# The normalised input's high and low halves are transposed by two transfers, and the products with the high half come first

## The chip, the core and the metric

One Trainium2 chip, one of its cores. The time is the device time of one execution in microseconds (us). Of a kernel that is run several times it is the median; the profile is of one execution by itself.

## What is computed

A layer of a vision tower over 64 batches of 128 tokens with 1024 channels. The token part (a state space kernel) gives h; around the change stands the attention:

```python
h = _L0_tok_ref(L0_tok_log_dt, L0_tok_Lambda, x, 1024)
h = h + _L0_attn_ref(_layernorm(h, axis=-1), L0_attn_Wq, L0_attn_Wk, L0_attn_Wv, L0_attn_Wo)
h = h + _L0_ffn_ref(_layernorm(h, axis=-1), L0_ffn_A, L0_ffn_B, L0_ffn_Wr, L0_ffn_br)
...
q = (x @ Wq).reshape(b, t, N_HEADS, HEAD_DIM).transpose(0, 2, 1, 3)
k = (x @ Wk).reshape(b, t, N_KV, HEAD_DIM).transpose(0, 2, 1, 3)
v = (x @ Wv).reshape(b, t, N_KV, HEAD_DIM).transpose(0, 2, 1, 3)
```

`_layernorm` is (x - mean) / sqrt(var + 1e-5). Then come a rotary embedding, causal softmax over 128 tokens in 32 heads with 8 key heads, the output projection Wo, and a low-rank feed forward with a router of 8.

## The kernel before, in words

The first stage (`s4_stage`) makes h of all batches in DRAM, as h0, and leaves the weights in SBUF, each as the sum of two 16-bit parts, high and low (`wq_hi`, `wq_lo`). It ends at about 260 us of the span. The second stage (`layer_stage`) runs over the 64 batches with a pipeline written out by hand: every engine has a function `body(i, odd)` that lists its steps for turn i, and `bodies` runs it for i from -3 to 66. A step names the batch it serves, so turn i works on batches i - 3 to i + 3 at once, and each engine takes its steps strictly in this order. Before a step, `reached(engine, semaphore, per, b, k)` waits until the semaphore stands at per x b + k. A step for a batch that doesn't exist is left out.

The way of batch b up to its products:

- SP loads h0 of the batch into `h_ln` (`load_ln`, L761); one buffer. It waits until both halves of the low part of batch b - 1 are made (`xl_done[0]`, L764).
- DVE takes the statistics (`norm1_stats`), ACT and DVE the root, ACT normalises in place (`norm_apply`) and writes the high part, the 16-bit copy, to `xs[0][:, 0, :]` (`x_high`, L1045). DVE writes the low part, what the copy leaves, to `xs[0][:, 1, :]` in two steps of 512 columns (`x_low`, L1195). Half 0 of batch i + 3 is DVE's last step of turn i, after `kv_rotate(i + 2)` and `q_rotate(i + 2, 0)`, which wait for TensorE's products of batch i + 2; half 1 is in the next turn.
- SP transposes both parts by one DMA of 128 x 2048 into `xt[odd]` (`x_transpose`, L779, issued at L785): blocks 0 to 7 of it are the high part, 8 to 15 the low one.
- TensorE multiplies: `kv` (L886) into the PSUM bank `pa`, `q_half` (L896) into `pb` and `pc`. Each is 24 products of 512 columns, in `products` (L849): for every k of 0 to 7 x_high w_hi, x_high w_lo and x_low w_hi. The body gives them out in ranges of k between other work: scores, values, the output projection `wo_half`, the feed forward.

Scores need `qt` and `kt`, the transposed queries and keys. The probabilities of a group of four heads go from ACT (`exps`) over POOL (`normalise`) to ACT (`p_high`) and POOL (`p_low`), both parts are transposed by SP (`p_transpose`, 128 x 1024, into `pt`), and TensorE multiplies them with the values.

All of the stage's DMAs are issued by SP, in one queue. Its turn, L824:

```python
def body(i, odd):
    load_res(i - 1)
    p_transpose(i - 1, 6)
...
    x2_transpose(i - 2)
    load_ln(i + 3)
    p_transpose(i, 2)
    p_transpose(i, 3)
    x_transpose(i + 2, odd)
    q_transpose(i + 1, 0)
    p_transpose(i, 4)
    p_transpose(i, 5)
    k_transpose(i + 1, 0)
    store(i - 3)
```

Of the kernel before, what the change touches and what calls it, by code (L numbers as in the profile page):

```python
# [26 lines left out]
KC = D // P  # L27
# [591 lines left out]
def layer_stage(nc, h0, out, W):  # L619
# [5 lines left out]
    with ExitStack() as ctx:  # L625
# [3 lines left out]
        def sem(name):  # L629
            return ctx.enter_context(nc.semaphore(name))  # L630
# [11 lines left out]
        xs = [sb(f"xs{i}", [P, 2, D], f16) for i in range(2)]  # L642
        xt = [sb(f"xt{i}", [P, 2 * KC, P], f16) for i in range(2)]
# [36 lines left out]
        pv_ps, pa, pb, pc, pd, tx = (ps(n) for n in ("pv_ps", "pa", "pb", "pc", "pd", "tx"))  # L680
# [2 lines left out]
        ln_in = sem("ln_in")  # L683
        res_in = sem("res_in")
        out_sent = sem("out_sent")
        xt_in = sem("xt_in")
        x2t_in = sem("x2t_in")
        qt_in = [sem(f"qt_in{i}") for i in range(2)]
        kt_in = [sem(f"kt_in{i}") for i in range(2)]
# [3 lines left out]
        kv_done = sem("kv_done")  # L693
        q_done = sem("q_done")
# [36 lines left out]
        def has(b):  # L731
            return not isinstance(b, int) or 0 <= b < NB

        def reached(eng, s, per, b, k=0):

            if isinstance(b, int):
                if b < 0 or per * b + k == 0:
                    return
                if b >= NB:
                    b, k = NB, 0  # L740
            eng.wait_ge(s, per * b + k)
# [13 lines left out]
        with nc.Block() as block:  # L755
            @block.sync
            def _(sp):
                def row(ap, b):
                    return ap[bass.ds(b, 1), :, :].rearrange("b t d -> (b t) d")

                def load_ln(b):  # L761
                    if not has(b):
                        return
                    reached(sp, xl_done[0], 2, b)  # L764
                    sp.dma_start(h_ln[:, :], row(h0, b)).then_inc(ln_in, 16)

                def load_res(b):
                    if not has(b):
                        return
                    reached(sp, h1_done, 2, b)  # L770
                    sp.dma_start(h_res[:, :], row(h0, b)).then_inc(res_in, 16)

                def store(b):
                    if not has(b):
                        return
                    reached(sp, h2_done, 2, b, 2)
                    sp.dma_start(row(out, b), h2[:, :]).then_inc(out_sent, 16)

                def x_transpose(b, odd):  # L779
                    if not has(b):  # L780
                        return
                    reached(sp, xl_done[0], 2, b, 2)
                    reached(sp, q_done, 2, b - 2, 2)
                    reached(sp, kv_done, 1, b - 2, 1)
                    sp.dma_start_transpose(xt[odd][:, :, :],  # L785
                                           xs[0][:, :, :].rearrange("p a d -> p (a d)")).then_inc(xt_in, 16)

                def x2_transpose(b):
                    if not has(b):
                        return  # L790
                    reached(sp, xl_done[1], 2, b, 2)
                    reached(sp, low_done, 1, b)
                    sp.dma_start_transpose(x2t[:, :, :],
                                           xs[1][:, :, :].rearrange("p a d -> p (a d)")).then_inc(x2t_in, 16)

                def q_transpose(b, half):
                    if not has(b):
                        return
                    reached(sp, qd_done, 2, b, half + 1)
                    reached(sp, s_done, G, b - 1, G // 2 * (half + 1))  # L800
                    heads = slice(H // 2 * half, H // 2 * (half + 1))
                    sp.dma_start_transpose(qt[:, heads, :],
                                           qs[:, heads, :, :, :].rearrange("p h a b d -> p (h a b d)")
                                           ).then_inc(qt_in[half], 16)

                def k_transpose(b, half):
                    if not has(b):
                        return
                    reached(sp, kd_done, 1, b, 1)
                    reached(sp, s_done, G, b - 1, G // 2 * (half + 1))  # L810
                    groups = slice(G // 2 * half, G // 2 * (half + 1))
                    sp.dma_start_transpose(kt[:, groups, :],
                                           ks[:, groups, :, :, :].rearrange("p g a b d -> p (g a b d)")
                                           ).then_inc(kt_in[half], 16)

                def p_transpose(b, g):
                    if not has(b):
                        return
                    reached(sp, pl_done, G, b, g + 1)
                    pb_, pg = group(b, g - RP)  # L820
                    reached(sp, pv_done, G // 4, pb_, pg // 4 + 1)
                    sp.dma_start_transpose(pt[g % RP][:, :, :], p16[g % 2][:, :]).then_inc(pt_in[g % RP], 16)
# [4 lines that stand above are left out]
                    p_transpose(i - 1, 7)  # L827
                    k_transpose(i, 1)
                    q_transpose(i, 1)
                    p_transpose(i, 0)  # L830
                    p_transpose(i, 1)
                    x2_transpose(i - 2)
                    load_ln(i + 3)
                    p_transpose(i, 2)
                    p_transpose(i, 3)
                    x_transpose(i + 2, odd)
                    q_transpose(i + 1, 0)
                    p_transpose(i, 4)
                    p_transpose(i, 5)
                    k_transpose(i + 1, 0)  # L840
                    store(i - 3)


                bodies(sp, body)
                sp.wait_ge(out_sent, 16 * NB)

            @block.tensor
            def _(pe):
                def products(bank, x, name, cols, k0, k1):  # L849

                    w_hi, w_lo = W[name + "_hi"], W[name + "_lo"]
                    for k in range(k0, k1):
                        pe.matmul(bank, x[:, k, :], w_hi[:, k, cols], start=(k == 0), stop=False)  # L853
                        pe.matmul(bank, x[:, k, :], w_lo[:, k, cols], start=False, stop=False)  # L854
                        last = pe.matmul(bank, x[:, KC + k, :], w_hi[:, k, cols], start=False, stop=(k == KC - 1))  # L855
                    return last

                def scores(b, g):
# [27 lines left out]
                def kv(b, odd, k0, k1):  # L886
                    if not has(b):
                        return
                    if k0 == 0:
                        reached(pe, h1_done, 2, b - 3, 1)  # L890
                        reached(pe, xt_in, 16, b, 16)
                    last = products(pa[:, :], xt[odd], "wkv", slice(0, 512), k0, k1)
                    if k1 == KC:
                        last.then_inc(kv_done, 1)

                def q_half(b, odd, half, k0, k1):  # L896
                    if not has(b):
                        return
                    if k0 == 0 and half == 0:
                        reached(pe, h1_done, 2, b - 3, 2)  # L900
                    if k0 == 0 and half == 1:
                        reached(pe, q_used, 2, b - 1, 2)
                    if k0 == 0:
                        reached(pe, xt_in, 16, b, 16)
                    last = products((pb, pc)[half][:, :], xt[odd], "wq",
                                    slice(512 * half, 512 * half + 512), k0, k1)
                    if k1 == KC:
                        last.then_inc(q_done, 1)

# [86 lines left out]
            def _(act):  # L996
# [48 lines left out]
                def x_high(w, b):  # L1045
                    if not has(b):
                        return
                    reached(act, ln_x[w], 1, b, 1)
                    reached(act, (xt_in, x2t_in)[w], 16, b)
                    A.activation(xs[w][:, 0, :], (h_ln, xn)[w][:, :], ACT.Copy).then_inc(xh_done[w], 1)  # L1050

                def q_high_a(b):
# [82 lines left out]
            def _(dve):  # L1135
# [59 lines left out]
                def x_low(w, b, half):  # L1195
                    if not has(b):
                        return
                    reached(dve, xh_done[w], 1, b, 1)
                    cols = slice(HALF * half, HALF * half + HALF)
                    V.tensor_tensor(xs[w][:, 1, cols], (h_ln, xn)[w][:, cols], xs[w][:, 0, cols],  # L1200
                                    ALU.subtract).then_inc(xl_done[w], 1)
# [259 lines left out]
```

## Time and profile before

| | |
|---|---|
| median of 3 runs | 2426.91 us (2426.84 to 2429.64) |
| profiled execution, its own time | 2428.1 us |
| its span | 2426.3 us |
| busy: TensorE (PE) | 2293.9 us, 95% |
| busy: VectorE (DVE) | 1983.9 us, 82% |
| busy: ScalarE (ACT) | 1835.2 us, 76% |
| busy: GpSimd (POOL) | 1711.2 us, 71% |
| DMA queue of SP, share of 16 engines | 92.0% |

PE is TensorE's matmul side, PEld its weight loads, SPq SyncE's queue of DMA issues. Busy is the time in which at least one instruction of the engine ran; matmuls overlap, so a matmul's duration (0.38 us) is longer than the distance to the next. The mean over the span mixes two stages, so it doesn't say what bounds either. The chain that ended last is TensorE for 68% of the span, in the pieces L853, L854 and L855, which are the lines of `products`, with 7% each for the banks pa and pb; ACT and DVE have 7% each. "Issue to landing" of a DMA runs from its issue on SP to its last byte; the span of the issue itself on SPq is separate, and with a full queue it is longer.

### The profile page before, as it was taken

To read this page: it belongs to the slowest core of one execution; us is meant where nothing else is said; L and a number is where in the kernel's file an instruction comes from. 1 tells how busy PE (TensorE), PEld (TensorE's weight loads), DVE (VectorE), ACT (ScalarE), POOL (GpSimd) and SP (SyncE) were. 2 spreads that over 40 slices of the span, in tenths; PEclk is the share of its full clock that TensorE was granted. 3 is DMA by queue.
4 is the path that set the end of the run, shared out by engine and by line. 5 is a ranking of instruction groups with operands and counts; after the bars stand their busy time and mean duration, and the time that the engine had idled before them with its cause. 6 is when DMAs were issued, how large, how long until landed. Compare 5 with 4: busy or idle time off the path is not lost.

```text
span 2426.3 us, 58560 instructions
## 1 busy us (share of the span) xinstructions
PE 2293.9 (95%) x18704; PEld 1247.0 (51%) x18704; DVE 1983.9 (82%) x7796; ACT 1835.2 (76%) x6270; POOL 1711.2 (71%) x1529
## 2 busy tenths in 40 slices
PE   2999589999999999999999999999999999999986
PEld 2777245555555555555555555555555555555543
DVE  8999468888888888888888888888888888888864
ACT  5988278777777777777777777777877777777773
POOL 1444187777777777777777777777777777777772
PEclk9999799999999999999999999999999999999998
DMA  2888489999999999999999999999999999999985
GB/s 76 263 253 235 114 149 179 190 186 183 190 185 184 186 190 186 181 189 188 186 182 188 186 180 189 190 181 190 187 187 182 186 191 181 190 190 186 181 163 110
DMA packets 1199524, 443.63 MB, mean 183 GB/s; under 512 B 1149552, under 2 KB 1151856, under 8 KB 1199216
## 3 DMA queue, kind: packets, MB, share of 16 engines
q1 hardware_dynamic: 1199216, 439.89, 92.0%
q8 instruction: 149, 2.44, 0.4%
q14 instruction: 159, 1.30, 0.2%
HBM read 87.42 MB, written 67.11 MB: 64 GB/s over the span
## 4 chain that ended last, share of the span: by engine, by line
PE 68%; ACT 7%; DVE 7%; DMA 3%; issue 3%; POOL 1%; SPq 0%; POOLq 0%; ACTq 0%; DVEq 0%
PE pb L853 7%; PE pa L853 7%; PE pb L854 7%; PE pb L855 7%; PE pa L854 7%; PE pa L855 7%; ACT pr L1005 5%; PE s_ps L867 4%; PE pc L854 4%; PE pc L855 4%; PE pc L853 4%; PE pv_ps L882 3%; DMA pt<-p 2%; PE pd L853 1%; PE pd L855 1%
## 5 line engine op out<-in xcount | busy, mean ns | idle before, releaser
L1005 ACT ACTIVATE pr<-pr,smin 128x128 f32<-128x128 f32 x2048 | 796.5, 391 | 191.1 <-DVE smin L1146 190.9
L1351 POOL TENSOR_TENSOR pr<-pr,rinv 128x512 f32<-128x512 f32 x512 | 577.6, 1138 | 358.4 <-DVE rinv L1154 347.2
L1359 POOL TENSOR_TENSOR p<-pr,p 128x512 f16<-128x512 f32 x512 | 590.7, 1159 | 115.5 <-ACT p L1015 109.2
L1146 DVE CUSTOM_DVE_ANT_0 pr<-s_ps,cst 128x128 f32<-128x128 f32 x2048 | 471.4, 287 | 150.2 <-POOL p L1359 108.2
L1015 ACT ACTIVATE p<-pr 128x512 f16<-128x512 f32 x512 | 320.0, 625 | 169.6 <-POOL pr L1351 147.9
L1005 ACT ACTIVATION_READ_ACCUMULATOR pr<-pr,smin 128x1 f32 x2048 | 386.4, 189 | 0.0
L612 PE MATMUL hps<-z,xw 128*128 128x256 f32 x848 | 194.1, 389 | 62.5 <-POOL xw L322 42.1
L853 PE MATMUL pa<-wkv_hi,xt 128*128 128x512 f16 x512 | 195.0, 381 | 27.4 <-DMA xt<-xs 27.4
L612 PEld LDWEIGHTS hps<-z,xw 128*128 128x128 f32 x848 | 163.1, 195 | 93.0 <-POOL xw L322 50.5
L867 PE MATMUL s_ps<-kt,qt 128*128 128x128 f16 x2048 | 199.1, 220 | 8.9 <-issue 4.5
L867 PEld LDWEIGHTS s_ps<-kt,qt 128*128 128x128 f16 x2048 | 149.5, 98 | 107.0 <-DVE smin L1146 5.7
L853 PE MATMUL pb<-wo_hi,ctx_t 128*128 128x512 f16 x512 | 195.1, 381 | 3.9 <-DVE rt_s L1212 1.9
L853 PE MATMUL pa<-wo_hi,ctx_t 128*128 128x512 f16 x512 | 195.3, 382 | 2.2 <-DVE ctx_t L1160 1.7
L853 PE MATMUL pb<-wq_hi,xt 128*128 128x512 f16 x512 | 195.6, 382 | 0.0
L854 PE MATMUL pb<-wq_lo,xt 128*128 128x512 f16 x512 | 195.5, 382 | 0.0
L855 PE MATMUL pb<-wq_hi,xt 128*128 128x512 f16 x512 | 195.3, 381 | 0.0
L854 PE MATMUL pa<-wkv_lo,xt 128*128 128x512 f16 x512 | 195.1, 381 | 0.0
L855 PE MATMUL pa<-wkv_hi,xt 128*128 128x512 f16 x512 | 195.1, 381 | 0.0
L854 PE MATMUL pa<-wo_lo,ctx_t 128*128 128x512 f16 x512 | 194.6, 380 | 0.0
L854 PE MATMUL pb<-wo_lo,ctx_t 128*128 128x512 f16 x512 | 194.6, 380 | 0.0
L855 PE MATMUL pb<-wo_hi,ctx_t 128*128 128x512 f16 x512 | 194.6, 380 | 0.0
L855 PE MATMUL pa<-wo_hi,ctx_t 128*128 128x512 f16 x512 | 194.5, 380 | 0.0
(192 smaller groups left out, 5559.4 us busy)
## 6 DMA issues: line engine op xcount, KB each, us to landing
h<-hout SPq DMA_DIRECT2D x128, 256.0 KB, 3.5
h_ln<-h SPq DMA_DIRECT2D x64, 512.0 KB, 4.2
h_res<-h SPq DMA_DIRECT2D x64, 512.0 KB, 4.6
out<-h SPq DMA_DIRECT2D x64, 512.0 KB, 3.2
pt<-p SPq DMA_TRANSPOSE x512, 3.9
xa<-x SPq DMA_DIRECT2D x16, 256.0 KB, 4.0
xb<-x SPq DMA_DIRECT2D x32, 128.0 KB, 3.7
wst<-wq SPq DMA_DIRECT2D x8, 512.0 KB, 5.7
```

The costliest lines, as they stand in the source:

```text
L612: last = pe.matmul(hps[t % 4][:, QROW * i:QROW * i + QROW], xw[w % XWR][:, t % WIN, 2 * i:2 * i + 2, :], z[g % ZR][:, 2 * (t % 2) + m, :], ...
L853: pe.matmul(bank, x[:, k, :], w_hi[:, k, cols], start=(k == 0), stop=False)
L854: pe.matmul(bank, x[:, k, :], w_lo[:, k, cols], start=False, stop=False)
L855: last = pe.matmul(bank, x[:, KC + k, :], w_hi[:, k, cols], start=False, stop=(k == KC - 1))
L867: last = pe.matmul(s_ps[g % 2][:, j * P:(j + 1) * P], qt[:, HG * g + j, :], kt[:, g, :], start=True, stop=True)
L882: last = pe.matmul(pv_ps[j * HD:(j + 1) * HD, to], v[:, g * HD:(g + 1) * HD], pt[g % RP][:, lo + j, :], start=(n == 0), stop=(n == 2))
L1005: last = A.activation(p, p, ACT.Exp, bias=smin[g % 2][:, j:j + 1], scale=-1.0, accum_out=rsum[g % 2][:, j:j + 1])
L1015: A.activation(p16[g % 2][:, 0:HG * P], pr[g % 2][:, :], ACT.Copy).then_inc(ph_done, 1)
L1146: V.tensor_tensor_reduce(pr[g % 2][:, cols], s_ps[g % 2][:, cols], mask, 1.0, 3e38, ALU.add, ALU.min, smin[g % 2][:, j:j + 1]).then_inc(ma ...
L1351: nc.gpsimd.tensor_tensor(p3, p3, rinv[g % 2][:, :].unsqueeze(2).broadcast_to([P, HG, P]), ALU.mult).then_inc(p_norm, 1)
L1359: nc.gpsimd.tensor_tensor(p[:, HG * P:], pr[g % 2][:, :], p[:, 0:HG * P], ALU.subtract).then_inc(pl_done, 1)
```

## The change

The transfer of 128 x 2048 becomes two of 128 x 1024, with a semaphore each (`xth_in`, `xtl_in`). The high one waits for `xh_done` in place of `xl_done`. Both stand on SP where the one stood. For `kv` and `q_half` a new function `x_products` takes the place of `products`: the same 24 products in another order, first the 16 with the high part (w_hi and w_lo for each k), then the 8 with the low part. The places in the body stay, with as many products each; product 0 waits for the high transfer, product 16 for the low one. ACT's `x_high` waits for the high transfer of the batch before, DVE's `x_low` now for the low one. `wo_half` and `low` still use `products`.

```diff
-        xt_in = sem("xt_in")
+        xth_in = sem("xth_in")
+        xtl_in = sem("xtl_in")
...
-                def x_transpose(b, odd):
+                def x_high_transpose(b, odd):
+                    if not has(b):
+                        return
+                    reached(sp, xh_done[0], 1, b, 1)
+                    reached(sp, q_done, 2, b - 2, 2)
+                    reached(sp, kv_done, 1, b - 2, 1)
+                    sp.dma_start_transpose(xt[odd][:, 0:KC, :], xs[0][:, 0, :]).then_inc(xth_in, 16)
+
+                def x_low_transpose(b, odd):
                     if not has(b):
                         return
                     reached(sp, xl_done[0], 2, b, 2)
                     reached(sp, q_done, 2, b - 2, 2)
                     reached(sp, kv_done, 1, b - 2, 1)
-                    sp.dma_start_transpose(xt[odd][:, :, :],
-                                           xs[0][:, :, :].rearrange("p a d -> p (a d)")).then_inc(xt_in, 16)
+                    sp.dma_start_transpose(xt[odd][:, KC:, :], xs[0][:, 1, :]).then_inc(xtl_in, 16)
...
-                    x_transpose(i + 2, odd)
+                    x_high_transpose(i + 2, odd)
+                    x_low_transpose(i + 2, odd)
...
+                def x_products(b, bank, x, name, cols, j0, j1):
+
+                    w_hi, w_lo = W[name + "_hi"], W[name + "_lo"]
+                    for n in range(3 * j0, 3 * j1):
+                        if n == 0:
+                            reached(pe, xth_in, 16, b, 16)
+                        if n == 2 * KC:
+                            reached(pe, xtl_in, 16, b, 16)
+                        k, w = (n // 2, (w_hi, w_lo)[n % 2]) if n < 2 * KC else (n - 2 * KC, w_hi)
+                        last = pe.matmul(bank, x[:, k if n < 2 * KC else KC + k, :], w[:, k, cols],
+                                         start=(n == 0), stop=(n == 3 * KC - 1))
+                    return last
...
-                        reached(pe, xt_in, 16, b, 16)
-                    last = products(pa[:, :], xt[odd], "wkv", slice(0, 512), k0, k1)
+                    last = x_products(b, pa[:, :], xt[odd], "wkv", slice(0, 512), k0, k1)
...
-                    if k0 == 0:
-                        reached(pe, xt_in, 16, b, 16)
-                    last = products((pb, pc)[half][:, :], xt[odd], "wq",
-                                    slice(512 * half, 512 * half + 512), k0, k1)
+                    last = x_products(b, (pb, pc)[half][:, :], xt[odd], "wq",
+                                      slice(512 * half, 512 * half + 512), k0, k1)
...
-                    reached(act, (xt_in, x2t_in)[w], 16, b)
+                    reached(act, (xth_in, x2t_in)[w], 16, b)
...
+                    if w == 0:
+                        reached(dve, xtl_in, 16, b)
```

SP's queue at the start of the second stage, batches 0 and 1, before:

```order
L765 DMA h_ln<-h 128x1024
L765 DMA h_ln<-h 128x1024 [waits xl_done0]
L785 DMA_TRANSPOSE xt<-xs 128x16x128 [waits xl_done0]
L765 DMA h_ln<-h 128x1024 [waits xl_done0]
L785 DMA_TRANSPOSE xt<-xs 128x16x128 [waits xl_done0]
L802 DMA_TRANSPOSE qt<-qs 128x16x128 [waits qd_done]
```

and now:

```order
L766 DMA h_ln<-h 128x1024
L766 DMA h_ln<-h 128x1024 [waits xl_done0]
L786 DMA_TRANSPOSE xt<-xs 128x8x128 [waits xh_done0]
L794 DMA_TRANSPOSE xt<-xs 128x8x128 [waits xl_done0]
L766 DMA h_ln<-h 128x1024 [waits xl_done0]
L786 DMA_TRANSPOSE xt<-xs 128x8x128 [waits xh_done0]
L794 DMA_TRANSPOSE xt<-xs 128x8x128 [waits xl_done0]
L810 DMA_TRANSPOSE qt<-qs 128x16x128 [waits qd_done]
```

Each transpose is two, the first waits for the high part alone, and the load of h_ln that waits for the low part stands ahead of both, as it stood ahead of the one.

TensorE's queue, batch 0, the rows up to the first uses of the low part (31 products are ahead of the first row that waits for xtl_in, none of which reads the low part), now:

```order
L876 MATMUL pb<-wq_hi,xt 128x512
L876 MATMUL pb<-wq_lo,xt 128x512
L876 MATMUL pb<-wq_hi,xt 128x512
L876 MATMUL pb<-wq_lo,xt 128x512
L876 MATMUL pb<-wq_hi,xt 128x512 [waits xtl_in]
L876 MATMUL pb<-wq_hi,xt 128x512
L876 MATMUL pa<-wkv_lo,xt 128x512
L876 MATMUL pa<-wkv_hi,xt 128x512 [waits xtl_in]
L876 MATMUL pa<-wkv_hi,xt 128x512 x7
```

Before, the third product of the batch (`L855 MATMUL pa<-wkv_hi,xt`) already read the low part, and the one wait was for the whole transfer.

## Rows read from the trace of the kernel before

**Rows 1.** Waits of TensorE, whole span: us in total, times, longest us.

```profile
PE pa L853 <- DMA xt<-xs: 27.4, 3, 21.8
```

**Rows 2.** Busy time by stretch: PE, PEld, DVE, ACT, POOL, clock, DMA share, GB/s.

```profile
420.00:2300.00 1880.00, 1874.20 (x16055) 970.87 (x16053) 1572.88 (x6734) 1461.61 (x5118) 1449.15 (x1324) 1.00 0.99 186
```

**Rows 3.** Timeline of TensorE, 262 to 345: start us, us, instruction [idle before <-releaser].

```profile
278.40 0.61 PE L853 MATMUL pa<-wkv_hi,xt 128*128 128x512 f16 x1 [21.85 <-DMA xt<-xs]
...
295.41 0.38 PE L854 MATMUL pc<-wq_lo,xt 128*128 128x512 f16 x1
295.63 0.38 PE L855 MATMUL pc<-wq_hi,xt 128*128 128x512 f16 x1
300.11 0.61 PE L853 MATMUL pa<-wkv_hi,xt 128*128 128x512 f16 x1 [4.10 <-DMA xt<-xs]
...
307.88 0.39 PE L867 MATMUL s_ps<-kt,qt 128*128 128x128 f16 x4
...
327.65 0.61 PE L853 MATMUL pa<-wkv_hi,xt 128*128 128x512 f16 x1 [1.41 <-DMA xt<-xs]
```

**Rows 4.** Timeline of SP's DMA issues, 272 to 345: start us, us of the issue.

```profile
272.59 0.33 SPq L765 DMA_DIRECT2D h_ln<-h  x1
272.97 3.54 SPq L785 DMA_TRANSPOSE xt<-xs  x1
...
303.97 2.50 SPq L812 DMA_TRANSPOSE kt<-ks  x2
...
323.26 1.69 SPq L785 DMA_TRANSPOSE xt<-xs  x1
```

**Rows 5.** Landing of single DMAs issued at 272.97, 323.26, 314.32 and 303.97.

```profile
xt<-xs SPq DMA_TRANSPOSE x1, 5.4
xt<-xs SPq DMA_TRANSPOSE x1, 4.3
pt<-p SPq DMA_TRANSPOSE x1, 3.2
kt<-ks SPq DMA_TRANSPOSE x1, 2.4
```

**Rows 6.** The page's DMA issues: count, median us from issue to landing.

```profile
pt<-p SPq DMA_TRANSPOSE x512, 3.9
...
xt<-xs SPq DMA_TRANSPOSE x64, 4.6
```

**Rows 7.** Timeline of VectorE, 262 to 345.

```profile
289.57 0.42 DVE L1222 TENSOR_SCALAR vf<-pa 128x256 f32<-128x256 f32 x1 [10.20 <-PE pa L855]
...
292.13 2.36 DVE L1200 TENSOR_TENSOR xs<-h_ln,xs 128x512 f16<-128x512 f32 x2
```

**Rows 8.** Timeline of SP's DMA issues, 1196 to 1236, in the steady part.

```profile
1199.33 2.98 SPq L785 DMA_TRANSPOSE xt<-xs  x1
1202.84 3.07 SPq L802 DMA_TRANSPOSE qt<-qs  x1
1206.67 2.61 SPq L822 DMA_TRANSPOSE pt<-p  x2
```

**Rows 9.** Timeline of TensorE, 1205 to 1212.

```profile
1208.16 0.38 PE L853 MATMUL pa<-wkv_hi,xt 128*128 128x512 f16 x1
```

**Rows 10.** SP's issues of pt and xt: issue ns min/median/max, first and last start.

```profile
L822 SPq DMA_TRANSPOSE pt<-p x512: 1231/1260/3512, 314.3 to 2388.8; - x171
L785 SPq DMA_TRANSPOSE xt<-xs x64: 1334/2532/3611, 273.0 to 2311.0; - x64
```

**Rows 11.** Busy time by stretch, three after a wait; columns as in rows 2.

```profile
278.40:282.20 3.80, 3.80 (x9) 1.35 (x10) 0.69 (x4) 2.44 (x3) 0.00 (x0) 0.50 0.00 0
...
300.10:302.60 2.50, 2.49 (x6) 0.89 (x7) 1.47 (x4) 0.29 (x2) 0.95 (x1) 0.50 0.47 90
...
325.10:333.10 8.00, 6.51 (x29) 2.53 (x30) 5.28 (x25) 5.63 (x23) 7.43 (x8) 0.50 1.17 183
```

**Rows 12.** Waits, 420 to 2300: us in total, times, longest us.

```profile
ACT p L1015 <- DMA pt<-p: 16.3, 30, 1.6
```

## The prediction

> **What bounds the kernel now.** I began with TensorE's part of the list of waits, because the change moves the release of products. TensorE waited for xt three times in the whole run, 27.4 us in all, 21.8 us of it once [rows 1]. Next the busy time by stretches: from 420 to 2300 us TensorE is busy 1874.20 of 1880.00 us at granted clock 1.00 [rows 2]. So in the steady part TensorE is the bound, nothing there waits for xt, and what an earlier xt can give lies before 420 us, in the fill of the pipeline. The timeline of TensorE shows the three waits: it starts batch 0 at 278.40 after 21.85 us idle, ends its last product at about 296.0 (295.63 + 0.38; a new one every 0.22 us), starts batch 1 at 300.11 after 4.10 idle, reaches the first scores at 307.88 and starts batch 2 at 327.65 after 1.41 idle [rows 3]. A start that comes earlier there should be kept to the end, since a full TensorE follows.
>
> **The queue.** The title of the change says that each part goes out when it is made. In SP's order it does not, but for batch 63, the last: load_ln of the next batch stands ahead of the high transpose and waits for both halves of the low part, xl_done. The order rows show it, and the timeline too: the load of h_ln is issued at 272.59 and the transpose at 272.97, directly behind it [rows 4]. I cost the two low subtractions at no gain, therefore. What is left is that the products need only the first half of the transfer.
>
> **The half transfer.** Batch 0's transfer took 5.4 us to land, behind a 512 KB load, batch 2's 4.3 with no load directly ahead; a pt of exactly the half's size (128x1024 f16) took 3.2 in the same stretch, a kt of half that again 2.4 [rows 5]. So g, the gain of a high part, is 4.3 - 3.2 = 1.1 us. Bounds: 4.6 - 3.9 = 0.7 by the medians of all [rows 6], and 5.4 - 3.2 = 2.2 if the half also escapes what the load ahead costs. I take 1.1, as the pair of one stretch and one state of the queue is nearest; the load stays ahead of either form. The Trainium skill speaks against the split (DMA: Bandwidth & Descriptors, section Anatomy of one DMA — SWDGE (gpsimd) path): about 2.0 us of every transfer are fixed and the rest is bytes over 436 GB/s. That makes an estimate of 262144 / 436e3 = 0.6 us for g, and 1.8 us in the sum below; these rows, of another issuing path, show a larger slope.
>
> **How it adds up.** *Batch 0*: TensorE starts g earlier, 1.1. The low part is out of reach: the order rows put 31 products ahead of the first that needs it, at least 31 x 0.22 = 6.8 us, and it lands about 1.3 us behind the high one. *Batch 1*: its two low subtractions stand on DVE behind the rotations of batch 0, which began at 289.57 when TensorE had its keys and values (10.20 us idle for them); they end at 294.5 (292.13 + 2.36) [rows 7], and the load and the transpose go out at once. All of that moves by 1.1, and its own half gives another 1.1: 2.2. The scores at 307.88 need kt too, issued at 303.97 and landed at 306.4 [rows 4, 5]; it moves by 1.1 to 305.3, the scores by 2.2 to 305.7, so 2.2 passes. With g = 2.2, kt would be last (304.2) and only 3.7 would pass. *Batch 2*: its transpose at 323.26 stands behind pt transfers that follow from those scores and moves by 2.2; its half adds 1.1, which the 1.41 us of idle time allows [rows 3]. Sum 3.3 us. By the lower bound 3 x 0.7 = 2.1; by the upper 3.7 + 1.41 = 5.1.
>
> **What it costs.** In the steady part I cost the earlier high part at nothing: xt is issued at 1199.33 and lands after some 4.6, 1203.9 [rows 8, 6], TensorE takes it at 1208.16 [rows 9]. That 4.2 us is also the cover of the low part, which TensorE first needs 30 products later still. One issue more per batch occupies SP: a pt issue has a median of 1.26 us, an xt issue 2.53 [rows 10], so two halves (2.52) fill what the whole fills now. If the queue is less full the whole takes its least, 1.33, and the split costs 2 x 1.23 - 1.33 = 1.13 more. Behind it stand q_transpose of half 0 and p_transpose 4 and 5. At 1202.31 SP is free, waits 0.53 to the qt issue and 0.76 to the pt pair [rows 8], together 1.29: it absorbs 1.13. The three waits per batch for the low part, and the other order of the same 72 products, I cost at nothing: the same bytes, the same weight loads, the same pitch, and waits on work that landed long before; from below, nothing in it can be a gain. ScalarE's wait for the earlier batch's xt gets weaker and VectorE's new one is for a transfer that landed a batch before: nothing.
>
> The profiled execution took 2428.1 us, 1.2 above the median of 2426.91, so 2428.1 - 3.3 = 2424.8 for it and **2423.6 us** for the median. About 0.2%, 4.85 us, is what a measurement of this kernel can tell from no change: my forecast, 0.14%, is below it.
>
> **Rivals.**
> *The clock takes it (0.12).* After each of the three waits the granted clock is 0.50, the lower level of 1.2 GHz: from 278.4 to 282.2, 300.1 to 302.6 and 325.1 to 333.1 [rows 11]. If the rise comes at the same instants whatever the start, an earlier start buys products of 0.42 us each (3.80 us for 9 [rows 11]) where 0.22 is the pace later: half the gain, 1.65 us, 2425.3. For it: the slow stretches have three lengths, 3.8, 2.5 and 5.5 us from the start of the products. Against: over executions the phase should even out. The rule would be that of the Trainium skill (TensorE: Matmul & The Clock Gate, Part 1): the activity window is free-running and does not reset with the kernel; the trace's three lengths agree.
>
> *More than the forecast (0.27).* The half lands in 3.2 behind the load also, 5.1 in all, and the idle time of 4.10 before batch 1, cut to 3 or less, no longer drops the clock: six products [rows 11] at 0.42 instead of 0.22 were 1.2 us. Together 6.3, 2420.6 us. For it: an xt issue behind the load takes 3.54 us of SP against 1.69 without [rows 4], which a shorter transfer may not pay. Against: those bytes of the load are ahead of both.
>
> *The queue pays (0.09), slower.* Where SP has no slack behind xt, the 1.13 us reach p_transpose 4 and 5, and ScalarE's copy for group 6, which reuses the buffers, waits. ScalarE waited for a pt 30 times in 62 batches, 16.3 us [rows 12]; if each of these hands on 1.13 and TensorE runs dry with it, 34 us, less 3.3: 2457.6 us. It decides from the point where the added issue is over the 1.29 us. Against: the full queue that makes the median 2.53, and TensorE's 99.7%.
>
> *That the change doesn't do what it says* holds for the early issue, and is in the forecast; if a high part did overtake the load, each of the first batches would gain its subtractions (1.3 us) too, which belongs to the second rival.
>
> **The numbers.** Forecast 0.52, rivals 0.12, 0.27, 0.09. The forecast and the clock rival are both within 0.2%: 0.64. Faster 0.27, slower 0.09. The range takes the first three cases: down to 2418.5, the second rival with 2 us for a clock that rises earlier after batch 2's start; up to 2429.5, no gain and the highest run shown, 2429.64. The slower rival is left out.
>
> **What would show it.** Each xt half issued directly behind the load, high landing in 3 to 4.3 us; the waits of TensorE for xt near 20.8, 3.0 and 0.3; batch 1 starting near 297.9, scores near 305.7, batch 2 near 324.4; the stretch from 420 unchanged at 0.997 busy. A high transpose issued before the subtractions, a steady part that is not within some 2 us of 1880 for the same work, or ScalarE's waits for pt well over 16 us would prove me wrong.

## The result, and the profile after

| | median, us | lowest to highest, runs | ratio to before, 95% interval |
|---|---|---|---|
| before | 2427.67 | 2424.74 to 2430.94, 20 | |
| the change | 2423.70 | 2421.61 to 2428.62, 20 | 0.9985, 0.9979 to 0.9991 |

The change is faster by 0.15%, some 3.6 us, with an interval of 2.2 to 5.1 us: real, since the interval is clear of 1, but smaller than the 0.2% that the prediction took as its bound. The profiled execution took 2426.01 us, 2.1 less than that of before.

The waits of TensorE after the change, whole span; us in total, times, longest us:

```profile
PE pa L876 <- DMA xt<-xs: 23.7, 3, 20.1
```

They were 27.4, 3 and 21.8 [rows 1]. The busy time by stretch, columns as in rows 2:

```profile
420.00:2300.00 1880.00, 1875.39 (x16115) 972.46 (x16114) 1575.27 (x6746) 1459.34 (x5125) 1449.42 (x1326) 1.00 0.99 186
```

TensorE is as full in the steady part as before (1874.20 [rows 2]), so the change is to be looked for in the fill. SP's DMA issues there, 262 to 345:

```profile
273.62 1.36 SPq L786 DMA_TRANSPOSE xt<-xs  x1
275.03 1.84 SPq L794 DMA_TRANSPOSE xt<-xs  x1
295.16 0.34 SPq L766 DMA_DIRECT2D h_ln<-h  x1
295.54 1.24 SPq L786 DMA_TRANSPOSE xt<-xs  x1
...
323.45 1.25 SPq L786 DMA_TRANSPOSE xt<-xs  x1
324.82 1.28 SPq L794 DMA_TRANSPOSE xt<-xs  x1
```

The high half still stands directly behind the load of h_ln, as the order said. How long the three high halves took to land, single DMAs issued at 273.62, 295.54 and 323.45:

```profile
xt<-xs SPq DMA_TRANSPOSE x1, 4.4
xt<-xs SPq DMA_TRANSPOSE x1, 4.3
xt<-xs SPq DMA_TRANSPOSE x1, 3.3
```

The whole ones had taken 5.4, 5.2 and 4.3 (the first and the last are [rows 5]): g, the gain of a half, is 1.0, 0.9 and 1.0 us. TensorE's timeline:

```profile
278.02 0.61 PE L876 MATMUL pa<-wkv_hi,xt 128*128 128x512 f16 x1 [20.14 <-DMA xt<-xs]
...
299.93 0.39 PE L876 MATMUL pa<-wkv_hi,xt 128*128 128x512 f16 x1 [3.29 <-DMA xt<-xs]
...
308.10 0.39 PE L889 MATMUL s_ps<-kt,qt 128*128 128x128 f16 x4
...
326.77 0.61 PE L876 MATMUL pa<-wkv_hi,xt 128*128 128x512 f16 x1 [0.26 <-DMA xt<-xs]
```

This execution reached its second stage later than the one of before: the first transpose is issued at 273.62 against 272.97 [rows 4], 0.65 us. Counted from that issue, batch 0 starts 1.03 us earlier than before, batch 1 0.83, the first scores 0.43, and batch 2 1.53 (53.15 us behind the issue, where it was 54.68). Of 2.2 us at batch 1 most is missing, and the busy time of three stretches says why:

```profile
278.00:283.50 5.50, 5.48 (x13) 1.94 (x14) 1.36 (x7) 2.70 (x4) 0.00 (x0) 0.50 0.06 14
301.00:304.30 3.30, 3.30 (x9) 1.21 (x8) 1.25 (x3) 0.73 (x2) 1.89 (x2) 0.50 0.72 135
325.90:331.40 5.50, 5.24 (x19) 2.00 (x16) 3.20 (x20) 3.94 (x15) 5.50 (x6) 0.50 1.15 181
```

After the first wait the granted clock stayed at 0.50, the lower level, for over 5.5 us of products, not 3.8 [rows 11]: 14 products of 0.42 us by the timeline where before had 9, and 5 x 0.21 us is the 1.03. VectorE's keys and values of batch 0 therefore came no earlier, 16.59 us behind the issue where it was 16.60 (289.57 [rows 7]):

```profile
290.21 0.42 DVE L1243 TENSOR_SCALAR vf<-pa 128x256 f32<-128x256 f32 x1 [10.17 <-PE pa L876]
```

What batch 1's start gained is its own half alone. Its first products ran at full pace, the clock fell at 301.0, and 8 were slow where before had 6: 0.42 us less, which leaves the 0.43 of the scores. In this one execution some half of the 3.3 us had not arrived at batch 2's start. From the first transpose to the end of the span it gained 2.75 us (2150.58, where it was 2153.33), so more arrived behind that.

### The profile page after: what moved, and what is told of

Read it like the earlier page. It is cut to its first block, busy times and chain, and to the rows that moved or that the text cites. A ratio compares the mean times of both kernels' runs of the same rounds, so it can differ in the third digit from the quotient of the medians.

```text
span 2424.2 us, 58812 instructions
## 1 busy us (share of the span) xinstructions
PE 2296.6 (95%) x18704; PEld 1248.9 (52%) x18704; DVE 1984.5 (82%) x7796; ACT 1829.6 (75%) x6270; POOL 1708.7 (70%) x1529
## 4 chain that ended last, share of the span: by engine, by line
PE 74%; DVE 4%; ACT 4%; DMA 2%; issue 2%; POOL 1%; SPq 0%; POOLq 0%; ACTq 0%; DVEq 0%
PE pc L876 12%; PE pb L876 11%; PE pa L876 11%; PE pb L862 4%; PE pa L862 4%; PE pb L864 4%; PE pb L863 4%; PE s_ps L889 4%; PE pa L863 4%; PE pa L864 4%; PE pv_ps L904 4%; ACT pr L1024 3%; PE pd L862 1%; PE pd L864 1%; PE pd L863 1%
## 5 line engine op out<-in xcount | busy, mean ns | idle before, releaser
L876 PE MATMUL pa<-wkv_hi,xt 128*128 128x512 f16 x1024 | 327.0, 381 | 23.7 <-DMA xt<-xs 23.7
L876 PE MATMUL pb<-wq_hi,xt 128*128 128x512 f16 x1024 | 327.9, 381 | 0.0
L876 PE MATMUL pc<-wq_hi,xt 128*128 128x512 f16 x1024 | 315.0, 379 | 0.0
L876 PE MATMUL pb<-wq_lo,xt 128*128 128x512 f16 x512 | 196.3, 383 | 0.0
L876 PE MATMUL pa<-wkv_lo,xt 128*128 128x512 f16 x512 | 196.0, 383 | 0.0
L876 PE MATMUL pc<-wq_lo,xt 128*128 128x512 f16 x512 | 194.0, 379 | 0.0
```

The source lines that it names most:

```text
L876: last = pe.matmul(bank, x[:, k if n < 2 * KC else KC + k, :], w[:, k, cols], start=(n == 0), stop=(n == 3 * KC - 1))
```

## The experiments

Each ratio is to the kernel before, run on the same chip. The kernels ran 11 times each, but e4 4, e5 6, e7 9 and e9 5 times.

| | us, median | ratio | 95% interval |
|---|---|---|---|
| e1, split, old order | 2429.18 | 1.0007 | 0.9998 to 1.0016 |
| e2, split for batches 0 to 2 | 2425.16 | 0.9986 | 0.9977 to 0.9994 |
| e3, split from batch 3 on | 2427.09 | 0.9999 | 0.9990 to 1.0008 |
| e4, high part ahead of the load | 2453.77 | 1.0105 | 1.0091 to 1.0119 |
| e5, the change, products ahead of batch 0 | 2421.79 | 0.9973 | 0.9962 to 0.9985 |
| e8, before, products ahead of batch 0 | 2428.45 | 1.0000 | 0.9991 to 1.0009 |
| e9, as e4 for batches 0 to 2 alone | 2420.66 | 0.9968 | 0.9956 to 0.9981 |
| e7, e9 and e5 together | 2422.33 | 0.9976 | 0.9967 to 0.9986 |
| e6, four transfers | 2426.56 | 0.9996 | 0.9987 to 1.0005 |
| e10, high part directly behind the load | 2427.55 | 1.0000 | 0.9991 to 1.0008 |

### Is it the half? e1

```diff
                         if n == 0:
                             reached(pe, xth_in, 16, b, 16)
-                        if n == 2 * KC:
                             reached(pe, xtl_in, 16, b, 16)
-                        k, w = (n // 2, (w_hi, w_lo)[n % 2]) if n < 2 * KC else (n - 2 * KC, w_hi)
-                        last = pe.matmul(bank, x[:, k if n < 2 * KC else KC + k, :], w[:, k, cols],
+                        k, m = n // 3, n % 3
+                        last = pe.matmul(bank, x[:, KC + k if m == 2 else k, :], (w_hi, w_lo, w_hi)[m][:, k, cols],
```

> The transfer is split as in the change, but the products stand in the old order (high, high, low for each k) and wait for both transfers, so nothing starts on the half. Half-transfer theory: the gain is gone; TensorE's three waits for xt add up to about 27 us as before, and the time is that of before within 1 us (2426.7 to 2428.7 where before has 2427.7). Rival, that the gain comes from two shorter transfers or from the new order's other waits: it keeps the 4 us. If two issues cost SP time in the steady part, this one is slower than before.

TensorE's waits for xt are back, and the gain is gone:

```profile
PE pa L875 <- DMA xt<-xs: 27.6, 3, 21.6
```

Two transfers alone give nothing. The median lies 1.4 us over before, outside the 1 us that was expected, but the interval of the ratio holds 1.

### Where is it? e2 and e3

Both let chosen batches keep one transfer; e2 reads as follows, e3 has `3 <= b < 64` for `0 <= b < 3`, and the waits count accordingly.

```diff
                 def x_high_transpose(b, odd):
-                    if not has(b):
+                    if not has(b) or not 0 <= b < 3:
                         return
...
+                    if not 0 <= b < 3:
+                        sp.dma_start_transpose(xt[odd][:, :, :],
+                                               xs[0][:, :, :].rearrange("p a d -> p (a d)")).then_inc(xtl_in, 16)
+                        return
                     sp.dma_start_transpose(xt[odd][:, KC:, :], xs[0][:, 1, :]).then_inc(xtl_in, 16)
```

> Only batches 0, 1 and 2 have two transfers; from batch 3 on one transfer of 128 x 2048 as before, with the high products first. Start theory: all of the change's gain is in the fill, so this one is as fast as the change, 0.9985 of before (0.998 to 0.999). Rival, that the steady part gains or loses by the split: it differs from the change.

> The mirror image: batches 0 to 2 have one transfer, batches 3 to 63 two. Start theory: ratio to before 1.000 (0.9995 to 1.0005), TensorE's waits for xt back at 27 us, and from 420 to 2300 us it is busy 1874 to 1876 us. Rival, that the queue pays for 61 more issues: over 1.0005.

Three batches of 64 carry all of it: 0.9986 against the change's 0.9985, and 0.9999 for the other 61. In e3 TensorE's waits for xt were 26.4 us (27 expected), and its busy time from 420 to 2300 was 1876.14 (1874 to 1876). e3 also has the new order of the products in all batches, with one transfer in the first three: the order alone gives nothing either. With e1 it leaves the products that start on the first half as the cause. e2's timelines, SP's first transpose and then TensorE, are also the ones that show the sum as it was worked out:

```profile
272.48 1.36 SPq L786 DMA_TRANSPOSE xt<-xs  x1
```

```profile
276.69 0.61 PE L883 MATMUL pa<-wkv_hi,xt 128*128 128x512 f16 x1 [19.98 <-DMA xt<-xs]
...
297.30 0.61 PE L883 MATMUL pa<-wkv_hi,xt 128*128 128x512 f16 x1 [3.33 <-DMA xt<-xs]
...
305.28 0.39 PE L896 MATMUL s_ps<-kt,qt 128*128 128x128 f16 x4
...
323.99 0.61 PE L883 MATMUL pa<-wkv_hi,xt 128*128 128x512 f16 x1 [0.37 <-DMA xt<-xs]
```

The three starts come 4.21, 24.82 and 51.51 us behind that issue. Before had 5.43, 27.14 and 54.68 [rows 3, 4]: gains of 1.2, 2.3 and 3.2 us, and 2.1 at the scores. At batch 0 this execution had 7 slow products, fewer than the 14 of the one above and the 9 of before, so two of them are part of what it gained behind batch 0's start, 0.4 us.

### The part that the change says and doesn't do: e4, e9 and e10

e4 puts the high transpose ahead of the load in SP's turn, so that it does go out when the high part is made. In the first batches nothing else then orders TensorE behind VectorE's reading of `pa` and `pb` (later `wo_half` waits for the same two steps ahead of it), so both get a wait:

```diff
+                    x_high_transpose(i + 2, odd)
                     load_ln(i + 3)
                     p_transpose(i, 2)
                     p_transpose(i, 3)
-                    x_high_transpose(i + 2, odd)
                     x_low_transpose(i + 2, odd)
...
+                        reached(pe, kv_used, 1, b - 1, 1)
...
+                        reached(pe, q_used, 2, b - 1, 1)
```

> The high transpose stands ahead of load_ln, so it really goes out when the high part is made; kv and q_half get a wait of their own for VectorE's reading of their banks, which the later transfer gave them so far. Order theory (the load ahead of it kept the change from doing what its title says): batch 0's high part goes out about 1.7 us earlier and lands in 3.2 instead of 4.4, TensorE starts some 2.9 us earlier; batch 1 starts directly behind batch 0 with no idle time (3.3 us now); the scores then wait for kt, which moves by 2.9. In all some 3 us under the change, 2420.7, ratio to before 0.9972. Rival, that kt, the clock or SP's order takes it: as the change, 0.9985. In the steady part nothing.

The fill did as expected: TensorE began batch 1 behind batch 0 with no wait, and waited 4.1 us for kt instead. Expected were 0.9972 and nothing in the steady part; the steady part lost what no theory of mine had, and the kernel is 26 us slower. Its busy time by stretch, its waits from 420 to 2300, and one turn of SP:

```profile
420.00:2300.00 1880.00, 1850.66 (x15812) 956.64 (x15811) 1550.28 (x6641) 1444.31 (x5051) 1428.06 (x1306) 1.00 0.98 184
```

```profile
ACT p L1036 <- DMA pt<-p: 56.7, 55, 3.4
DVE bn L1186 <- DMA h_ln<-h: 55.3, 52, 3.1
...
PE pb L862 <- DVE rt_s L1235: 23.7, 40, 1.3
...
PE pb L876 <- DVE h L1280: 0.8, 1, 0.8
```

```profile
1202.60 1.54 SPq L786 DMA_TRANSPOSE xt<-xs  x1
1204.19 0.57 SPq L766 DMA_DIRECT2D h_ln<-h  x1
```

In the change the first three of these waits are:

```profile
ACT p L1034 <- DMA pt<-p: 16.4, 30, 1.5
...
DVE bn L1184 <- DMA h_ln<-h: 2.6, 3, 1.8
...
PE pb L862 <- DVE rt_s L1233: 1.5, 2, 1.2
```

One issue ahead of the load makes it 1.5 us late in that turn; VectorE, in its fixed order, waits for it ahead of the rotations that free TensorE's bank. The added waits stand in front of L876, and TensorE waited there 0.8 us, once: they are not what costs. e9 keeps the early issue for batches 0 to 2 and leaves the rest as in the change, with the two waits in all batches:

```diff
+                    if i + 2 < 3:
+                        x_high_transpose(i + 2, odd)
                     load_ln(i + 3)
                     p_transpose(i, 2)
                     p_transpose(i, 3)
-                    x_high_transpose(i + 2, odd)
+                    if i + 2 >= 3:
+                        x_high_transpose(i + 2, odd)
                     x_low_transpose(i + 2, odd)
```

> The high transpose ahead of load_ln for batches 0 to 2 alone, from batch 3 on where the change has it; the two waits for VectorE's reading stay in for all batches. Load theory (with the high transpose ahead of it everywhere, the load came late in each batch, VectorE waited for h_ln 55 us and TensorE for VectorE's rotations 24): the steady part is back at 1875 us busy and the start keeps its 3.3 us, ratio to before 0.9971. Rival, that the two added waits on TensorE cost the 26 us: this one is slower than before too.

0.9968, the lowest ratio of the study, from five executions: 4 us under the change by the ratios, though their intervals meet. SP's issues and TensorE's first start and first scores in it:

```profile
261.43 0.35 SPq L766 DMA_DIRECT2D h_ln<-h  x1
...
269.97 1.36 SPq L786 DMA_TRANSPOSE xt<-xs  x1
271.39 0.56 SPq L766 DMA_DIRECT2D h_ln<-h  x1
272.00 1.24 SPq L794 DMA_TRANSPOSE xt<-xs  x1
281.22 1.23 SPq L786 DMA_TRANSPOSE xt<-xs  x1
289.95 0.33 SPq L766 DMA_DIRECT2D h_ln<-h  x1
```

```profile
273.18 0.61 PE L879 MATMUL pa<-wkv_hi,xt 128*128 128x512 f16 x1 [17.12 <-DMA xt<-xs]
...
302.03 0.39 PE L892 MATMUL s_ps<-kt,qt 128*128 128x128 f16 x4 [4.11 <-DMA kt<-ks]
```

The high part of batch 1 goes out at 281.22, 8.7 us ahead of the load of batch 2 at 289.95: that load waits for batch 1's low part, which stands on VectorE behind batch 0's rotations, while the high part needs only ScalarE's copy. From the first load of h_ln to the first scores it is 40.6 us here. In the change it is 44.8, from this load to 308.10:

```profile
263.34 10.23 SPq L766 DMA_DIRECT2D h_ln<-h  x2
```

e10 puts the high transpose behind the load, ahead of the two pt transfers, to part late load from late pt; it keeps the two waits on TensorE:

```diff
                     load_ln(i + 3)
+                    x_high_transpose(i + 2, odd)
                     p_transpose(i, 2)
                     p_transpose(i, 3)
-                    x_high_transpose(i + 2, odd)
                     x_low_transpose(i + 2, odd)
```

> The high transpose directly behind load_ln in every batch, ahead of p_transpose 2 and 3, with the two waits on TensorE. It parts the two consequences of standing ahead of the load, which cost 26 us: here the load is on time and only p_transpose 2 and 3 are later by one issue, 1.3 us. If the late load made the loss (VectorE's 55 us of waits for h_ln): ratio about 0.9985, VectorE's waits for h_ln back near 3 us. If the late pt did (ScalarE's waits for pt rose from 16 to 57 us): about 1.01 again.

```profile
420.00:2300.00 1880.00, 1871.53 (x16035) 969.18 (x16033) 1569.88 (x6724) 1458.91 (x5113) 1444.94 (x1323) 1.00 0.99 186
```

```profile
ACT p L1036 <- DMA pt<-p: 60.5, 75, 2.5
...
DVE bn L1186 <- DMA h_ln<-h: 9.8, 15, 1.3
```

Neither expectation was met: it is 1.0000, 3.6 us over the change and 25 under e4 by the ratios. ScalarE waits for pt as long as in e4 (60.5 and 56.7), VectorE hardly for h_ln. So the late pt costs some 4 us, and by difference the late load made most of e4's loss. The steady part says the same: from the store of batch 2 to that of batch 60 the profiles take 1888.6 us in the change, 1894.7 in e10 and 1916.1 in e4, and 1886.7 to 1891.7 in all others.

### How much room has the queue? e6

```diff
-                    sp.dma_start_transpose(xt[odd][:, 0:KC, :], xs[0][:, 0, :]).then_inc(xth_in, 16)
+                    for c in range(2):
+                        sp.dma_start_transpose(xt[odd][:, 4 * c:4 * c + 4, :],
+                                               xs[0][:, 0, HALF * c:HALF * c + HALF]).then_inc(xth_in, 16)
```

and the same for the low part; the waits count 32.

> Each of the two transfers is split once more, so a batch has four of 128 x 512 in place of two of 128 x 1024: two issues more on SP, which at the kt transposes' 1.19 to 1.23 us each makes 4 x 1.2 = 4.8 us where the change has 2.55. That is 2.25 us more, over the 1.29 us of slack behind xt that the prediction's slower rival decides by. Queue theory: the added issues now reach p_transpose 4 and 5; ScalarE's waits for pt rise well over 16 us, and the time is over that of the change, by up to 30 batches x 1 us. Rival, that SP's waits for POOL, 6 us per batch, absorb it all: ratio as the change, 0.9985.

```profile
L787 SPq DMA_TRANSPOSE xt<-xs x128: 1188/1260/2028, 272.5 to 2310.4; - x128
L797 SPq DMA_TRANSPOSE xt<-xs x128: 1193/1259/2302, 275.2 to 2313.0; - x128
```

```profile
1198.95 2.53 SPq L787 DMA_TRANSPOSE xt<-xs  x2
1201.59 2.52 SPq L797 DMA_TRANSPOSE xt<-xs  x2
1204.20 2.40 SPq L814 DMA_TRANSPOSE qt<-qs  x1
1206.69 3.04 SPq L834 DMA_TRANSPOSE pt<-p  x2
```

A quarter costs SP as much as a half, 1.26 us by the medians, so the four take 5.04. SP's two waits behind xt, 0.53 and 0.76 us [rows 8], are gone here, and ScalarE's waits for pt are 81.4 us in 88 times. The time is 0.9996, some 2.7 us over the change by the ratios, its interval overlapping the change's. From 420 to 2300:

```profile
420.00:2300.00 1880.00, 1867.69 (x16109) 971.45 (x16107) 1587.49 (x6743) 1463.11 (x5122) 1450.18 (x1325) 1.00 1.00 186
```

TensorE's busy time falls by 7.7 us, but it does as many products in the stretch (16109, where the change has 16115), and from the store of batch 2 to that of batch 60 e6 takes 1888.95 us, the change 1888.57. The first step of the slower rival exists, the longer wait for pt; that it costs time is not shown, and if it does, it is a tenth of the 34 us.

### The clock: e5, e8 and e7

e5 and e8 have these products ahead of the second stage's first turn, one in the change, one in the kernel before; e7 has them in e9. They are not part of the layer.

```diff
+                for n in range(56):
+                    pe.matmul(pd[:, :], W["wq_hi"][:, n % KC, 0:P], W["wo_hi"][:, n % KC, 0:512], start=True, stop=True)
                 bodies(pe, body)
```

> The changed kernel with 56 products more on TensorE ahead of batch 0, on weights and into a bank that nobody reads before it is written anew; they fill the idle time before batch 0's transfer. Clock theory (the low level after the wait takes part of what the early half gives): no product of batch 0 is slow, where the change's profile had 14 of them and before's 9; that is worth 9 to 14 x 0.21 = 1.9 to 2.9 us, ratio to before about 0.9976. Rival, that batch 0's products have slack: as the change, 0.9985.

> The kernel before with the same 56 products ahead of batch 0. Clock theory: 9 slow products less, 1.9 us, ratio to before 0.9992. The distance to the changed kernel with the same products is then the half transfer's gain without batch 0's clock: 3.3 us by the prediction, 0.0014 of the time.

> The last one with the 56 products ahead of batch 0. If both gains add up: 0.9971 less some 2 us, ratio to before 0.9963, 2418.7 us where before has 2427.7. If the scores of batch 0 are bound by kt and not by the products, less of it comes through, 0.9967.

No product of batch 0 was slow in any of the three. In e8 the first stretch of products is at full clock, and the next one, after the wait for batch 1, is at the lower level for longer than before's 2.5 us (from 297.24 to 301.9 at least):

```profile
277.40:282.00 4.60, 4.60 (x22) 2.11 (x23) 0.69 (x4) 2.50 (x3) 0.00 (x0) 1.00 0.00 0
296.00:301.90 5.90, 4.66 (x11) 1.64 (x12) 3.76 (x10) 1.03 (x3) 3.01 (x3) 0.50 0.58 113
```

The 1.9 us did not arrive: 1.0000 where 0.9992 was expected, an interval that holds both. Batch 1's start did come 1.8 us earlier, counted from the first transpose (25.38, where before had 27.14), but 12 of its products were slow, where before had 6, and the first scores are 0.4 us earlier. e5 has 0.9973 against an expected 0.9976, but e7, expected at 0.9963 or 0.9967, is not under e9 (0.9976 and 0.9968). Whether full clock for batch 0 is worth anything stays open: the three comparisons point both ways, by less than their intervals. The end of the run adds scatter of this size. From the store of batch 60 to the end of the span it is 42.4 us in before and 42.9 in e9, but 46.8 in e7 and 47.1 in e8, and the granted clock there is at the lower level for longer; in e7 and in e9:

```profile
2377.80:2391.30 13.50, 6.87 (x61) 3.08 (x62) 5.49 (x12) 4.06 (x7) 3.06 (x3) 0.50 0.63 159
```

```profile
2377.70:2387.70 10.00, 5.10 (x57) 2.38 (x58) 3.77 (x10) 3.83 (x6) 2.31 (x2) 0.50 0.87 210
```

## Why the prediction held

**The bound.** Right: the steady part is TensorE's, unchanged by the split (1874.20 and 1875.39 of 1880), and e3 puts a value of 0.9999 on 61 of the 64 batches.

**The queue's order.** Right, and it was what kept the forecast under 0.2%. But the second rival valued the early issue at the subtractions alone, 1.3 us a batch. In e9's profile it brings the first scores 4.2 us nearer to the first load, because batch 1's high part goes out 8.7 us ahead of the load that it stood behind. What that is worth in time is not settled: e9 against the change gives 4 us, e7 against e5, the same edit with the products ahead of batch 0 in both, gives nothing (0.9976 and 0.9973).

**The half transfer.** g was 1.1 and measured 1.0, 0.9 and 1.0. The second rival's half of 3.2 us behind the load did not come: it took 4.4 and 4.3 there. The Trainium skill's fit for transfers issued another way (DMA: Bandwidth & Descriptors, section Anatomy of one DMA — SWDGE (gpsimd) path), 2.0 us fixed and bytes over 436 GB/s, gives an estimate of 0.6; the trace does not agree for these transposes, whose half saves about 1.0.

**The sum.** 3.3 us was forecast, the ratio gives 3.6, and the medians 4.0. In the profiled pair batch 2's start gained 1.5 only, in e2's profile 1.2, 2.3 and 3.2 at the three starts, against 1.1, 2.2 and 3.3 forecast. That e2's starts fit so well is in part luck with the clock, and one profile of either kernel does not carry the sum; the 20 executions do. kt did not bind at the scores, as worked out; in e9, where the start was earlier still, it did (4.11 us).

**The cost.** Two halves took SP 1.28 + 1.28 us at the median where the whole took 2.53 [rows 10], and ScalarE's waits for pt were 16.4 us, 30 times, where they were 16.3 [rows 12]. Right at nothing. What was mis-sized is the rival's price, 34 us: with more than its threshold added (e6) the kernel lost some 3 us by ratios whose intervals overlap, and nothing that its steady part shows. ScalarE's waits for pt say little of the time: 81.4 us of them there, and 60.5 in e10, which lost 3.6.

**The clock.** The rival's loss is in the profile of the change, 5 slow products more behind the first wait. But one pair can't show that the earlier start caused it: in nine profiles TensorE comes to batch 0 out of this wait, and 7 to 14 of its products are slow, 14 in the change and 7 in e2, whose batch 0 has the same two transfers. Over 20 executions it did not keep the half, which is what the prediction held against it. The second rival's hope for batch 1 failed: an idle time of 3.29 us, cut from 4.10, was still followed by the lower level. The Trainium skill's rule (TensorE: Matmul & The Clock Gate, Part 1) is that the activity window is free-running; the trace agrees, in that the slow stretch behind the same wait has many lengths.

## What to carry to other kernels

Read the queue's order before you believe that a transfer is issued when its data are ready: here a load with a later condition stood ahead of it, and the list of waits did not name it. In a pipeline that is full in its steady part, an earlier operand pays only in the fill, once; it can be given to the first batches alone, and here should be, since one issue moved ahead of a load cost 26 us when all 64 batches had it. Judge a gain of a few us by many executions: one profile can show half of it.

## What was not expected of the hardware

The issue of these DMA transposes has a floor on SP that hardly falls with their size: 1.19 us at least for 128 x 512, 1.23 for 128 x 1024 and 1.33 for 128 x 2048 [rows 10], with medians of 1.26 for the first and 1.26 (pt) to 1.28 (xt) for the second. The landing falls with it: 4.3 us at the least for 128 x 2048, 3.1 for the half, 2.4 for the quarter. And the lower clock after a wait is not a fixed toll: behind the same wait it held for 7 to 14 products, and where it was gone at one wait (e8) 12 products were slow at the next, where before had 6.
